# A decoder on one core: both layers' threads merged into one order each, two heads per cross score product, tails by query tile

## The chip, the core and the metric

One Trainium2 chip, one of its cores. The metric is the device time of one execution in microseconds, the median of the runs shown. One profiled execution gives the trace from which every row here is taken.

## What is computed

x is 8 sequences of 256 tokens with 256 features; ctx is 8 sequences of 77 tokens with 192 features. There are two layers, each sublayer followed by a residual and a layer norm:

```python
x = _layernorm(x + _L0_attn_ref(x, ...))        # gated linear attention, 4 heads, keys 64, values 128
x = _layernorm(x + _L0_xattn_ref(x, ctx, ...))  # cross attention, 16 heads of 16: x0
x = _layernorm(x + _L0_ffn_ref(x, ...))         # 8 experts, the top 2 of each token, hidden size 512
x = _layernorm(x + _L1_attn_ref(x, ...))        # self attention, 16 heads, window of 128 keys to either side: s1
x = _layernorm(x + _L1_xattn_ref(x, ctx, ...))  # cross attention, scores clipped at +-10000: x1
x = _layernorm(x + _L1_ffn_ref(x, ...))         # 8 experts, top 2, with a capacity for each expert
```

## The kernel before

The eight sequences are four pairs; sequence p of a pair is thread p (0 or 1), with its own buffers and its own four of the eight PSUM banks, `bank(p, 0)` to `bank(p, 3)`. A thread is a list of named stages, and a stage is a function of each engine that takes part in it. `in_turns` weaves the two threads into one order by a written list of turns (so many stages of thread 0, so many of thread 1, and so on); `play` (L225) runs through it on every engine, which issues the instructions of its stages in just that order. So the order says what is queued behind a waiting instruction on each engine. There is an order for each pair: TURNS0 and TURNS1 for the first three of a layer, LAST0 and LAST1 for the last, with routing steps (choose, count, rank, hots, table, place, index, gather) put in between. Between the layers come the experts of layer 0, after layer 1 its own.

The stages of one attention (x0, s1 or x1; `c` is which): `k`, `v`, `q` projections on TensorE, copied with bias by VectorE (`kz`, `va`) and ScalarE (`qe`); `scores` on TensorE in units, each followed by `max` on VectorE (L874 for s1 in 4 units of 4 heads; L878 for a cross attention in 2 units of one query tile and 16 heads). `split` and `nmT` turn the maxima round, and `ST` (L1630) makes the scores again, transposed and shifted, for `exp` on ScalarE (L645); x1 has `clip` on VectorE (L895) and `shift` in between. Then the tail: `values` (L1658, TensorE), `OT` (L649, ScalarE copies 1024 columns), `untr` (L1666, transposed back, 8 transposes), `norm` (L901, L903, VectorE), `tout` (L1673, 4 transposes), `onT` (L653, ScalarE), `wo` (L1680, projection), `res` (L910 and layer norm moments L833 to L840, VectorE), `rstd` (L1388, GpSimd), `final` (L846, VectorE). Heads lie in rows of 32, four groups beside each other (`rows_of(r)`).

A cross score unit:

```python
for g in range(G):
    for r in range(RT):
        ins = mm(bank(p, r)[:, g * M:(g + 1) * M], b.q[rows_of(r), g // 2, u * P:(u + 1) * P], kz[rows_of(r), g // 2, g % 2, :],
                 start=(g == 0), stop=True, skip_group_check=True)
if p == 1 and u == 0:
    ins = idle(p, IDLE_SCORES, 0, G * M)
```

`idle` (L1566) issues products whose result nobody reads. They stand at the split, at the clip, before the turn of the gated attention (thread 1), before the router's logits and in the last turn of a layer, besides the place above.

In layer 0 the gated attention of the pair comes first (`g_...`: keys, values and gates L1728, scores L1750, mix L1758 to L1760, turn L1775, output L1783), and the keys of the next pair (`g_keys`) are made in the tail of the cross attention.

Of the kernel before, what the change touches and what calls it, by code (L numbers as in the profile page):

```python
# [11 lines left out]
ALU = mybir.AluOpType  # L12
ACT = mybir.ActivationFunctionType
# [53 lines left out]
class Attn:  # L67
# [14 lines left out]
    def scores_at(self, n):  # L82

        if self is X0:
            return NT * n
        return NT * PAIRS + (G + NT) * n + (0 if self.selfattn else G)

    def exps_at(self, n):

        if self is X0:  # L90
            return KC * n
        return KC * PAIRS + (G + KC) * n + (0 if self.selfattn else G)
# [24 lines left out]
def cross_stages(c, clip):  # L117

    out = [("k", c), ("kz", c), ("v", c), ("va", c), ("turn", c), ("xinT", c), ("q", c), ("qe", c), ("xb", c)]
    for t in range(NT):  # L120
        out += [("scores", c, t), ("max", c, t)]
    out += [("split", c), ("nmT", c), ("nmTe", c)]
    for k in range(KC):
        out.append(("ST", c, k))
        if clip:
            out += [("clip", c, k), ("shift", c, k), ("exp", c, k)]
        else:
            out.append(("exp", c, k))
# [3 lines left out]
def after_probs(c):  # L132
    return [(n, c) for n in ("values", "OT", "untr", "norm", "tout", "onT", "wo", "res", "rstd", "final")]

def self_stages(c):
    out = [("xb", c)]
    for g in range(G):
        out += [("scores", c, g), ("max", c, g)]
    out += [("split", c), ("nmT", c), ("nmTe", c)]  # L140
    for g in range(G):
        out += [("ST", c, g), ("exp", c, g)]
    return out + after_probs(c)
# [6 lines left out]
def lockstep(n, stages):  # L150

    return [(s, p, n) for s in stages for p in range(2)]

def in_turns(n, threads, turns, extra):

    out, at = [], [0, 0]
    for i, count in enumerate(turns):
        p = i % 2
        for stage, m in threads[p][at[p]:at[p] + count]:  # L160
            if m < PAIRS:
                out.append((stage, p, m))
            out += [((e,), 0, n) for e in extra.get((p, *stage), [])]
        at[p] += count
    assert at == [len(t) for t in threads]
# [3 lines left out]
TURNS0 = (3, 3, 4, 2, 3, 4, 2, 3, 4, 2, 3, 4, 5, 7, 4, 1, 2, 4, 4, 4, 2, 1, 4, 4, 1, 2, 2, 2, 2, 2, 2, 2, 2, 1, 2, 7, 6, 3, 5, 4)  # L169
TURNS1 = (3, 3, 2, 2, 1, 1, 2, 2, 5, 5, 5, 5, 2, 2, 2, 2, 2, 2, 3, 3, 2, 1, 3, 4, 1, 5, 6, 2, 2, 3, 3, 2, 3, 1, 3, 5, 3, 3, 1, 1, 3, 3, 2, 1, 2, 3, 8, 3, 3, 5, 4, 7, 4, 4)  # L170
LAST0 = (2, 2, 2, 2, 6, 6, 2, 2, 3, 2, 6, 5, 5, 1, 2, 1, 3, 8, 3, 1, 2, 5, 5, 6, 2, 2, 3, 2, 2, 2, 7, 5, 4, 7, 3, 3)
# [1953 lines left out]
```

## Time and profile before

| | us |
|---|---|
| median of 3 runs | 1130.51 |
| lowest and highest | 1126.09, 1133.84 |
| span of the profiled execution | 1131.2 |
| TensorE busy in it | 1010.0 (89%) |
| VectorE busy | 618.1 (55%) |
| ScalarE busy | 425.0 (38%) |
| GpSimd busy | 255.4 (23%) |
| mean granted TensorE clock | 0.967 |

Layer 0 with its four pairs goes to about 381 us, its experts to 597, layer 1 to 1027, the experts of layer 1 and the end to 1131.
### The profile page before, as it was taken

To read this page: it belongs to the slowest core of one execution; us is meant where nothing else is said; L and a number is where in the kernel's file an instruction comes from. 1 tells how busy PE (TensorE), PEld (TensorE's weight loads), DVE (VectorE), ACT (ScalarE), POOL (GpSimd) and SP (SyncE) were. 2 spreads that over 40 slices of the span, in tenths; PEclk is the share of its full clock that TensorE was granted. 3 is DMA by queue.
4 is the path that set the end of the run, shared out by engine and by line. 5 is a ranking of instruction groups with operands and counts; after the bars stand their busy time and mean duration, and the time that the engine had idled before them with its cause. 6 is when DMAs were issued, how large, how long until landed. Compare 5 with 4: busy or idle time off the path is not lost.

```text
span 1131.2 us, 20802 instructions
## 1 busy us (share of the span) xinstructions
PE 1010.0 (89%) x8612; PEld 719.1 (64%) x8612; DVE 618.1 (55%) x1398; ACT 425.0 (38%) x557; POOL 255.4 (23%) x282
## 2 busy tenths in 40 slices
PE   6889889999987899999998798879888987986997
PEld 3666566576575799997445465747565665654566
DVE  2653753662667564333334846675575668765443
ACT  1533533524433355555541254142416231541112
POOL 0310310120130233333322020231013110210662
PEclk9999999899897899999999899999999999997999
DMA  6013413211400691111113000200020010004447
GB/s 188 1 43 126 135 43 107 89 43 44 152 1 1 254 378 57 47 48 47 43 39 98 1 2 6 85 2 5 1 76 2 6 38 1 1 2 131 130 135 236
DMA packets 64237, 80.50 MB, mean 71 GB/s; under 512 B 12736, under 2 KB 57680, under 8 KB 63120
## 3 DMA queue, kind: packets, MB, share of 16 engines
q1 hardware_dynamic: 53392, 61.15, 16.3%
q0 software_dynamic: 5664, 15.47, 4.2%
q10 hardware_dynamic: 5088, 2.56, 0.9%
q8 instruction: 68, 1.11, 0.4%
q14 instruction: 25, 0.20, 0.1%
HBM read 46.13 MB, written 33.03 MB: 70 GB/s over the span
## 4 chain that ended last, share of the span: by engine, by line
PE 61%; DVE 17%; ACT 12%; issue 5%; DMA 2%; POOL 2%; SPq 0%; ACTq 0%; DVEq 0%; POOLq 0%
PE ps L1522 8%; PE ps L1857 7%; DVE sb_arena L874 6%; ACT sb_arena L645 6%; PE ps L1658 5%; PE ps L1680 4%; PE ps L1885 4%; PE ps L1868 3%; PE ps L1728 3%; PE ps L1783 3%; DVE sb_arena L878 3%; PE ps L1566 2%; PE ps L1995 2%; PE ps L1630 2%; PE ps L1905 2%
## 5 line engine op out<-in xcount | busy, mean ns | idle before, releaser
L645 ACT ACTIVATE sb_arena<-ps 77x2048 f32<-77x2048 f32 (+1 forms) x64 | 116.5, 1880 | 27.9 <-PE ps L1612 26.7
L1388 POOL TENSOR_TENSOR sb_arena<-sb_arena,sb_neghalf 128x2 f32<-128x2 f32 x40 | 28.7, 719 | 397.2 <-DVE sb_arena L840 397.2
L1522 PE MATMUL ps<-sb_arena,sb_wreg 128*128 128x256 f32 (+1 forms) x512 | 110.8, 365 | 6.8 <-issue 3.8
L1522 PEld LDWEIGHTS ps<-sb_arena,sb_wreg 128*128 128x128 f32 (+1 forms) x512 | 89.0, 195 | 23.7 <-issue 8.3
L1857 PE MATMUL ps<-sb_arena 128*128 128x128 f32 x800 | 100.2, 280 | 3.2 <-ACT sb_arena L757 2.3
L1630 PE MATMUL ps<-sb_arena 32*77 32x256 f32 (+1 forms) x1024 | 78.4, 424 | 25.8 <-ACT sb_arena L645 13.1
L1857 PEld LDWEIGHTS ps<-sb_arena 128*128 128x128 f32 x800 | 97.0, 196 | 5.2 <-ACT sb_arena L757 2.9
L757 ACT ACTIVATE sb_arena<-sb_arena 128x1024 f32 x72 | 76.0, 1057 | 16.8 <-issue 12.4
L1630 PEld LDWEIGHTS ps<-sb_arena 32*77 32x77 f32 (+1 forms) x1024 | 44.3, 177 | 46.1 <-ACT sb_arena L645 24.2
L874 DVE TENSOR_REDUCE sb_arena<-ps 128x8 f32<-128x2048 f32 x32 | 71.0, 2282 | 3.5 <-PE ps L1586 3.5
L1566 PE MATMUL ps<-sb_headrow,sb_identb 128*32 128x512 bf16 (+1 forms) x266 | 65.8, 385 | 1.4 <-DVE sb_arena L878 1.3
L1465 POOL DMA_INDIRECT outs<-sb_arena,sb_idx x36 | 35.5, 987 | 134.8 <-ACT sb_arena L743 134.8
L901 DVE RECIPROCAL sb_arena<-ps 128x32 f32<-128x32 f32 x24 | 8.6, 357 | 100.2 <-PE ps L1666 98.7
L635 ACT ACTIVATE sb_nmTb<-ps 128x256 bf16<-128x256 f32 x24 | 9.2, 383 | 143.5 <-PE ps L1604 143.5
L1658 PE MATMUL ps<-sb_arena,sb_va 77*32 77x256 f32 (+1 forms) x1024 | 58.5, 381 | 3.1 <-ACT sb_arena L645 2.5
L1728 PE MATMUL ps<-sb_wreg,sb_arena 128*128 128x512 f32 x128 | 60.7, 635 | 0.2 <-DVE sb_arena L926 0.2
L1409 POOL TENSOR_SCALAR_AFFINE_SELECT sb_arena<-sb_arena 128x512 f32<-128x512 f32 x48 | 29.6, 647 | 125.2 <-ACT sb_arena L645 125.2
L878 DVE TENSOR_REDUCE sb_arena<-ps 128x16 f32<-128x1232 f32 x32 | 45.4, 1438 | 21.1 <-PE ps L1591 21.0
L846 DVE TENSOR_SCALAR sb_arena<-sb_arena 128x256 f32<-128x256 f32 x80 | 39.2, 531 | 27.3 <-POOL sb_arena L1388 27.1
L1680 PE MATMUL ps<-sb_wreg,sb_arena 128*128 128x256 f32 x192 | 45.2, 384 | 5.7 <-ACT sb_arena L653 5.7
L1658 PEld LDWEIGHTS ps<-sb_arena,sb_va 77*32 77x32 f32 (+1 forms) x1024 | 31.2, 110 | 27.4 <-ACT sb_arena L645 8.7
L1583 PE MATMUL ps<-sb_arena 32*128 32x256 f32 x512 | 36.7, 400 | 13.2 <-DVE sb_arena L874 13.2
(285 smaller groups left out, 1886.9 us busy)
## 6 DMA issues: line engine op xcount, KB each, us to landing
sb_arena<-in_m_w SPq DMA_DIRECT2D x8, 1536.0 KB, 9.8
sent<-sb_xres SPq DMA_DIRECT2D x32, 256.0 KB, 2.6
sb_arena<-outs SPq DMA_DIRECT2D x16, 512.0 KB, 6.0
outs<-sb_zeros SPq DMA_DIRECT2D x4, 1664.0 KB, 9.7
sent<-sb_zeros SPq DMA_DIRECT2D x2, 2560.0 KB, 13.7
sb_arena<-in_m_w SPq DMA_DIRECT2D x16, 256.0 KB, 3.4
early<-sb_xres SPq DMA_DIRECT2D x12, 256.0 KB, 2.9
sb_arena<-in_xT SPq DMA_DIRECT2D x8, 256.0 KB, 3.2
```

The lines of the kernel that those rows point to most:

```text
L645: nc.scalar.activation(dst, src, ACT.Exp).then_inc(S(f"h_PT{p}"), 1)
L757: nc.scalar.activation(arena[:, to:to + 1024], arena[:, bass.ds(blk * WORDS + 1024 * part, 1024)], ACT.Copy).then_inc(S(signal), 1)
L874: v.tensor_reduce(b.nm[:, :, u].rearrange("p (t r) -> p r t", t=NT), bank(p, 0, RT).rearrange("p r (t k) -> p r t k", t=NT), axis=AX.X, op ...
L878: v.tensor_reduce(b.nm[:, u * RT:(u + 1) * RT, :], bank(p, 0, RT)[:, :, 0:G * M].rearrange("p r (g k) -> p r g k", g=G), axis=AX.X, op=ALU ...
L1522: ins = mm(dst[:, m * cols:(m + 1) * cols], wt[0:rows, k, m * P:(m + 1) * P], src[0:rows, k, 0:cols], start=(k == 0), stop=(k == KC - 1))
L1566: ins = mm(bank(p, n)[IDLE:P, first:], identb[:, IDLE:P], headrow[:, :, :].rearrange("p g k -> p (g k)")[:, first:], start=True, stop=True ...
L1630: ins = mm(bank(p, r)[0:c.keys, a * L:(a + 1) * L], key, b.q[rows_of(r), u // 2 if c.selfattn else u, :], start=(a == 0), stop=False, skip ...
L1658: ins = mm(bank(p, 2 + g // 2)[rows_of(r), (g % 2) * L:(g % 2 + 1) * L], b.va[0:c.keys, kt, g * RT + r, :], b.PT[0:c.keys, g, first:first ...
L1680: ins = mm(bank(p, 3)[:, t * D:(t + 1) * D], bufs[p].onT[:, k, t * P:(t + 1) * P], W[f"{c.name}_wo"][:, k, :], start=(k == 0), stop=(k == ...
L1728: ins = mm(bank(p, 2 + t), b.xT[:, k, t * P:(t + 1) * P], W[wt][:, k, :], start=(k == 0), stop=(k == KC - 1))
L1857: ins = mm(to[:, m * P:(m + 1) * P], w[:, k, m * P:(m + 1) * P], slots0[j % 2].xT[:, k, :], start=(k == 0), stop=(k == KC - 1))
L1885: ins = mm(to[rows, :], slots0[j % 2].xT[:, k, rows], weights_of(c, blk, at + FH * k, FH, at + FH * k), start=(k == 0), stop=(k == KC - 1) ...
```

## The change

Four things. A cross score product now takes the two heads that share a chunk of the query together, so that a unit has 8 products of 154 columns for 16 of 77, and the unread products after thread 1's first cross scores are gone. The stages from `values` to `res` are split in two: `values` and `OT` by half of the head groups, `untr`, `norm`, `tout`, `onT`, `wo` and `res` by query tile. For that the results of tile 1 lie in bank 2 (`result_bank`) and the turned tile 1 in bank 1 (`turned_bank`), and the keys of the next pair in layer 0 wait for the residual. Each layer has one order for all four pairs (`whole_thread`, TURNS0 with 330 turns and TURNS1 with some 450, mostly of one to three stages), and the routing steps are put at new places of it; the early count goes to thread 1 and its banks. The other unread products stay where they were; those of the last turn of a layer now wait for the residual.

```diff
-                    for g in range(G):
+                    for k in range(KC):
                         for r in range(RT):
-                            ins = mm(bank(p, r)[:, g * M:(g + 1) * M], b.q[rows_of(r), g // 2, u * P:(u + 1) * P], kz[rows_of(r), g // 2, g % 2, :],
-                                     start=(g == 0), stop=True, skip_group_check=True)
-                    if p == 1 and u == 0:
-                        ins = idle(p, IDLE_SCORES, 0, G * M)
+                            ins = mm(bank(p, r)[:, 2 * k * M:2 * (k + 1) * M], b.q[rows_of(r), k, u * P:(u + 1) * P],
+                                     kz[rows_of(r), k, :, :].rearrange("p a m -> p (a m)"), start=(k == 0), stop=True, skip_group_check=True)
...
 def after_probs(c):
-    return [(n, c) for n in ("values", "OT", "untr", "norm", "tout", "onT", "wo", "res", "rstd", "final")]
+    out = []
+    for i in range(2):
+        out += [("values", c, i), ("OT", c, i)]
+    for n in (("untr", "norm"), ("tout", "onT"), ("wo", "res")):
+        for t in range(NT):
+            out += [(x, c, t) for x in n]
+    return out + [("rstd", c), ("final", c)]
...
+def whole_thread(head, thread, p):
+
+    return head + [(stage, m) for n in range(PAIRS) for stage, m in thread(p, n) if m < PAIRS]
...
+        def turned_bank(p, t):
+
+            return bank(p, 1 if t else 2)[:, 0:KC * P].rearrange("p (k q) -> p k q", k=KC)
+
+        def result_bank(p, t):
+
+            return bank(p, 2 if t else 3)[:, 0:D]
...
+            def heads(p, n, c, i):
+                act.wait_ge(S(f"h_OT_done{p}"), 2 * c.at(n) + i + 1)
+                nc.scalar.activation(bufs[p].OT[:, 2 * i:2 * i + 2, :], halves(bank(p, 2 + i)), ACT.Copy).then_inc(S(f"h_OT{p}"), 1)
...
+            def norm(p, n, c, t):
+                b = bufs[p]
+                dve.wait_ge(S(f"h_O{p}"), NT * c.at(n) + t + 1)
+                o = bank(p, t).rearrange("p (h x) -> p h x", x=2 * DH)
+                v.reciprocal(b.rec[:, t, :], o[:, :, DH]).then_inc(S(f"h_on{p}"), 1)
+                dve.wait_ge(S(f"h_on{p}"), 2 * (NT * c.at(n) + t) + 1)
+                v.tensor_tensor(b.on[:, t, :].rearrange("p (h x) -> p h x", h=H), o[:, :, 0:DH],
+                                b.rec[:, t, :].unsqueeze(2).broadcast_to([P, H, DH]), ALU.mult).then_inc(S(f"h_on{p}"), 1)
+
+            def residual(p, n, c, t):
+                b = bufs[p]
+                dve.wait_ge(S(f"h_wo{p}"), NT * c.at(n) + t + 1)
+                if t == 0:
+                    dve.wait_ge(S(f"h_xb{p}"), c.at(n) + 1)
+                v.tensor_tensor(b.res[:, t, :], result_bank(p, t), b.xb[:, t, :], ALU.add).then_inc(S(f"h_res{p}"), 1)
+                dve.wait_ge(S(f"h_res{p}"), NT * c.at(n) + t + 1)
+                ins = v.bn_stats(b.st1 if t else b.st0, b.res[:, t, :])
+                if t + 1 == NT:
+                    ins.then_inc(S(f"h_moments{p}"), 1)
+                    moments("h", p, c.at(n))
...
             def turn_result(p, n, c):
                 if n + 1 == PAIRS and p == 0:
+                    pe.wait_ge(S(f"h_res{p}"), NT * (c.at(n) + 1))
                     idle(p, IDLE_RESULT, 2)
...
             def gla_keys(p, n):
                 b = bufs[p]
                 pe.wait_ge(S(f"a_in{p}"), 64 * (n + 1))
+                if n:
+                    pe.wait_ge(S(f"h_res{p}"), NT * X0.at(n))
```

TensorE's order in pair 1 of layer 0, from the turn of the gated attention to the first scores, was: k0, g_turn0, g_turn1, g_wo0, g_wo1, k1, v0, turn0, v1, q0, turn1, q1, scores0.0, scores1.0, scores0.1, scores1.1. It is: k0, g_turn0, g_wo0, g_turn1, v0, g_wo1, k1, turn0, v1, q0, turn1, scores0.0, q1, scores0.1, scores1.0, scores1.1. In the tail of x1 it was untr0, untr1, tout0, wo0, (turn of the next pair), tout1, wo1; it is untr0.0, untr0.1, untr1.0, tout0.0, untr1.1, tout0.1, wo0.0, wo0.1, tout1.0, tout1.1, wo1.0, (turn of the next pair), wo1.1.

## Rows read from the trace of the kernel before

**Rows 1.** By stage: length, busy PE, PEld, DVE, ACT, POOL, clock, DMA, GB/s
```profile
110.00:197.00 87.00, 79.61 (x648) 56.23 (x648) 44.40 (x91) 35.49 (x53) 15.56 (x14) 1.00 0.31 101
197.00:287.00 90.00, 83.42 (x643) 58.33 (x644) 44.25 (x90) 35.17 (x52) 15.57 (x14) 0.94 0.23 74
287.00:381.00 94.00, 82.46 (x644) 56.75 (x642) 66.38 (x194) 35.20 (x52) 18.12 (x17) 0.88 0.17 58
...
726.00:829.00 103.00, 89.86 (x1021) 62.09 (x1020) 64.41 (x113) 36.84 (x40) 17.68 (x24) 1.00 0.09 27
```

**Rows 2.** The chain that ended last, in order of time: start, length, what
```profile
625.06 15.49 DVE sb_arena L874 x7
...
659.53 7.16 PE ps L1658 x128
...
730.70 15.49 DVE sb_arena L874 x7
...
762.80 7.16 PE ps L1658 x128
```

**Rows 3.** Timeline of TensorE: the tail of S1 in pair 1
```profile
769.85 2.31 PE L1666 MATMUL ps<-sb_ident,sb_arena 128*128 128x128 f32 x16
...
773.83 3.62 PE L1680 MATMUL ps<-sb_wreg,sb_arena 128*128 128x256 f32 x16
777.28 1.01 PE L1522 MATMUL ps<-sb_arena,sb_wreg 96*128 96x77 f32 x8
```

**Rows 4.** Timeline of TensorE: the tail of X1 in pair 1
```profile
809.02 2.31 PE L1666 MATMUL ps<-sb_ident,sb_arena 128*128 128x128 f32 x16
...
812.63 1.99 PE L1680 MATMUL ps<-sb_wreg,sb_arena 128*128 128x256 f32 x8 [0.69 <-ACT sb_arena L653]
...
816.23 1.99 PE L1680 MATMUL ps<-sb_wreg,sb_arena 128*128 128x256 f32 x8 [0.74 <-ACT sb_arena L653]
818.06 1.89 PE L1522 MATMUL ps<-sb_arena,sb_wreg 128*128 128x256 f32 x8
```

**Rows 5.** Timeline of TensorE: cross scores and tail of X0, pair 1
```profile
155.20 1.99 PE L1522 MATMUL ps<-sb_arena,sb_wreg 128*128 128x256 f32 x8 [0.69 <-ACT sb_arena L624]
...
157.12 2.13 PE L1591 MATMUL ps<-sb_arena 32*128 32x77 f32 x64
...
175.25 2.31 PE L1666 MATMUL ps<-sb_ident,sb_arena 128*128 128x128 f32 x16
...
182.78 1.04 PE L1709 MATMUL ps<-sb_arena,sb_wreg 128*16 128x256 f32 x4
```

**Rows 6.** Timeline of TensorE: products of 32 rows and 256 columns
```profile
792.85 1.10 PE L1630 MATMUL ps<-sb_arena 32*77 32x256 f32 x16 [0.47 <-ACT sb_nmTb L635]
```

**Rows 7.** Timeline of VectorE: maxima of the cross scores, X0, pair 1
```profile
158.32 4.21 DVE L878 TENSOR_REDUCE sb_arena<-ps 128x16 f32<-128x1232 f32 x3 [1.99 <-PE ps L1591]
```

**Rows 8.** Groups by line and form, whole span: busy, mean ns, idle before
```profile
L649 ACT ACTIVATE sb_arena<-ps 128x1024 f32<-128x1024 f32 x24 | 24.6, 1023 | 28.1 <-PE ps L1658 28.0
...
L903 DVE TENSOR_TENSOR sb_arena<-ps,sb_arena 128x512 f32<-128x512 f32 x24 | 16.6, 691 | 0.8
...
L653 ACT ACTIVATE sb_arena<-ps 128x512 f32<-128x512 f32 x24 | 14.3, 596 | 29.6 <-PE ps L1673 29.6
...
L743 ACT ACTIVATE sb_arena<-ps 128x256 f32<-128x256 f32 x36 | 13.8, 383 | 75.7 <-PE ps L1868 46.3 <-PE ps L1905 29.3
...
L901 DVE RECIPROCAL sb_arena<-ps 128x32 f32<-128x32 f32 x24 | 8.6, 357 | 100.2 <-PE ps L1666 98.7
...
L1332 DVE TENSOR_TENSOR sb_arena<-ps,sb_arena 128x256 f32<-128x256 f32 x16 | 6.1, 420 | 8.3 <-PE ps L1995 8.3
```

**Rows 9.** Timeline of TensorE: unread products in layer 1's last turn
```profile
1027.21 2.76 PE L1566 MATMUL ps<-sb_headrow,sb_identb 128*32 128x512 bf16 x12
```

**Rows 10.** Timeline of TensorE: unread products before the turn, thread 1
```profile
139.10 1.04 PE L1566 MATMUL ps<-sb_headrow,sb_identb 128*32 128x512 bf16 x4
```

**Rows 11.** Busy time in a stretch of 4 us, columns as in group 1
```profile
644.00:648.00 4.00, 2.81 (x28) 1.91 (x32) 2.46 (x10) 3.97 (x4) 0.35 (x1) 0.57 0.00 0
```

More of the change, by code:

```diff
@@ L147, in self_head, with in_turns @@
     return [(n, c) for n in ("turn", "xinT", "k", "kz", "q", "qe", "v", "va")]
-def lockstep(n, stages):
-    return [(s, p, n) for s in stages for p in range(2)]
-def in_turns(n, threads, turns, extra):
+def in_turns(threads, turns, extra):
     out, at = [], [0, 0]
@@ L187, in first_thread @@
         of_pair(n, "o_turn", "o_T") + of_pair(n + 1, "g_decay", "g_z") + of_pair(n, "o_route", "o_logits", "store")
[L190 to L198 removed]
+def whole_thread(head, thread, p):
+    return head + [(stage, m) for n in range(PAIRS) for stage, m in thread(p, n) if m < PAIRS]
+LAST = PAIRS - 1
+EXTRA0 = {(1, 3, "g_sp"): ["choose"], (1, 3, "g_y"): ["count", "counts"], (0, 3, "g_wo"): ["rank"], (0, 3, "OT", X0, 1): ["hots"],
+          (1, 3, "OT", X0, 0): ["table"], (0, 3, "res", X0, 1): ["index"], (0, 3, "rstd", X0): ["place"], (1, 3, "norm", X0, 0): ["raw"],
+          (0, 3, "final", X0): ["turned"], (1, 3, "norm", X0, 1): ["first"], (0, 3, "o_turn"): ["blocks", "gather"]}
+EXTRA1 = {(0, 3, "kz", S1): ["choose"], (1, 3, "va", S1): ["count", "counts"], (0, 3, "values", S1, 0): ["rank"], (0, 3, "values", S1, 1): ["hots"],
+          (0, 3, "rstd", X1): ["place"]}
+def first_layer():
+    head = of_pair(0, "g_keys", "g_low", "g_decay", "g_z")
+    return in_turns([whole_thread(head, first_thread, p) for p in range(2)], TURNS0, EXTRA0)
 def second_thread(p, n):
@@ L443, in build_program @@
         order0 = first_layer()
[L444 to L445 removed]
+        order1 = second_layer()
         def rows_of(r):
@@ L777, in _ @@
             act.wait_ge(S("rescaled"), 3)
-            play(head1, stages)
-            for order in order1:
-                play(order, second)
+            play(order1, second)
             picks(3, 4)
@@ L1309, in _ @@
             scale_bias(["s1_bq", "x1_bq"], "rescaled")
-            play(head1, stages)
-            for order in order1:
-                play(order, stages | routing(1))
+            play(order1, stages | routing(1))
             choose_late(1)
@@ L1475, in store1 @@
                     unread(p)
-            play(head1, stages)
-            for order in order1:
-                play(order, stages | {"store": lambda p, n: store1(p, n)})
+            play(order1, stages | {"store": lambda p, n: store1(p, n)})
             def gather1(e):
```

167 lines of the change are left out of this document (67 added, 100 removed), and 16 rows, old and new, of tables (TURNS0, TURNS1).

## The prediction

> **What bounds the kernel now.** I read the busy time by stage first. In a pair of layer 1 (726 to 829 us) TensorE is busy 89.9 of 103 us, VectorE 64.4, ScalarE 36.8; in a pair of layer 0 (110 to 197 us) TensorE 79.6 of 87 [rows 1]. So TensorE is the engine to look at, but it waits 13 and 7 us in a pair, and the chain of work that ended last, in order of time, says for whom. From 730.70 us VectorE takes 15.49 us for seven of the eight S1 maxima (2.2 us each) and TensorE waits for it; then ScalarE runs eight exponentials of 1.9 us; the value products start at 762.80 us, and from there TensorE and the hand-overs between engines set the time [rows 2]. The edits don't touch the maxima or the exponentials. They touch the cross scores and what follows the values, so the sum is one of TensorE's waits there.
>
> The row that matters most is the tail, the stretch from the end of the values to the end of the output projection. In S1, pair 1, it runs from 769.85 to 777.28 us [rows 3]: 7.43 us. TensorE's own work in it is 16 transposes back (about 1.8), 8 transposes out (0.9) and 8 projections (773.83 to 777.28, 3.45), 6.2 us; 1.2 us is waiting for copies and normalisations. In X1 it runs from 809.02 to 818.06 us, 9.04 us [rows 4], for the same work and one early turn of the next pair (0.45): 6.7 us, so 2.3 us of waiting, of which 0.69 and 0.74 are named there. In X0 175.25 to 182.78 us, 7.53 us [rows 5].
>
> **Part 1, two heads per cross score product.** Each of the 32 score units (2 layers, 4 pairs, 2 threads, 2 query tiles) had 16 products of 77 columns and now has 8 of 154, with half the weight loads. Two units took 2.13 us in 64 records, 33 ns a record, 1.06 us a unit [rows 5]. A product of the same 32 rows with 256 columns takes 1.10 us for 16 records, 69 ns [rows 6]. On the line between them 154 columns take 48 ns, so 16 records take 0.77 us: 0.29 less. The bounds: nothing (the time goes by columns, which stay 1232) and 0.53 less (it goes by records). I take 0.29, because 77 columns lie close to the line's lower end and the price can't be wholly by columns when 3.3 times the columns cost 2.1 times the time. Most of it is hidden: VectorE needs 4.21 us for three maxima with nothing between [rows 7], longer than the scores either way. Only the first unit of a phase stands ahead of VectorE. So 0.29 in each of 8 phases. The 4 unread products after thread 1's first cross scores go as well; they ran while thread 0's maximum was on VectorE, so they are worth nothing here, but see the clock.
> The page "TensorE: Matmul & The Clock Gate" of the Trainium skill (LDWEIGHTS, loading the stationary operand) says that a weight load takes time by its columns, whatever its rows. By that the old unit is bound by its loads of 128 columns, and halving them would save the whole 0.53, 2 us more over the eight phases; no row here separates loads from products.
>
> **Part 2, tails by query tile.** Values, copy, transposes back, normalisation, transposes out, copy, projection and residual become two each. The work of TensorE stays. ScalarE's copy of OT, 1.02 us for 1024 columns, becomes two of 0.60; onT's 0.60 becomes two of 0.38; VectorE's 0.69 us operations on 512 columns become two of 0.42, the reciprocal of 0.36 two of between 0.18 and 0.36 [rows 8]. That adds 0.34 us of ScalarE and some 0.4 to 0.7 us of VectorE to each of 24 tails, 8 us and 10 to 17 us in all, beside TensorE's 6.2 us of work a tail. If that cover were gone, VectorE's part alone would be 0.7 us a tail.
> I set the new S1 tail on the old one's clock, t = 0 at 769.85. Thread 1's first OT copy is over while its second value half runs; the second copy ends at 0.75 instead of 1.15. Transposes back of thread 0 fill 0 to 0.9, of thread 1's tile 0 to 1.35. Thread 0's tile 0 is normalised at 1.3 (0.03 + 0.25 + 0.42 after 0.5), tile 1 at 2.05, thread 1's tiles at 2.75 and 3.5. Transposes out and projection follow each: thread 0's tile 0 is projected from 3.0, the four halves (0.87 each) and the last transposes end near 6.7. Old: 7.43. So 0.7 us a tail; what is late next, thread 1's final, has its residual and half of its statistics done earlier by the same amount, and the K and V products of X1 (3.4 us) still cover it. X0, the same from 7.53: 0.8. In X1 the new order also puts all of thread 0's tail before thread 1's transposes out, and thread 1's last projection after the early turn. The same working ends at 7.3 against 9.04: 1.7. The last pair is another matter: after its projection stand the place products and 12 unread products (2.76 us) that now wait for the residual first [rows 9], so what the tail gives is cut: 0.9.
>
> **Part 3, the merged orders.** Most of TensorE's sequence is the old one, as the two lists of stages for pair 1 show, read against each other. Two things differ in layer 0. The scores of thread 0 now stand ahead of thread 1's Q, in a wait of 0.69 us [rows 5]. By the durations in the rows its first maximum starts 2.5 us sooner than at 158.32; each thread's second maximum then waits for its own scores, 1.1 and 0.9 us, and the 0.3 us of the split fall into these waits: 0.75 is left at the end of the maxima. The output projection of the gated attention, thread 0, stands ahead of thread 1's four unread products and turn; these took 1.04 us inside a wait [rows 10] and are now in the way, and thread 0's projection waits 1.1 us for its copy: it costs about 0.5. The new waits (keys of the next pair on the residual, since its tile 1 lies in bank 2) are passed while thread 1's projections (1.8 us) run, the residual needing 0.5; g_low, decay and all of ScalarE's next pair are queued behind it and so don't move. DMA: no transfer is added; the loads still wait on the same events. The count moves to thread 1, inside VectorE's work in both layers: nothing. In the last pair of layer 0 the 64 one-hots and the table stay on VectorE ahead of thread 1's norm, but thread 0's exponentials and values pass ahead of thread 1's: I take the 1.05 of the other pairs and 0.75 more for this, a choice without a row of its own (its ends are nothing and one exponential, 1.9).
>
> **Sum.** Layer 0: 3 pairs x (0.75 - 0.5 + 0.8) = 3.2, last pair 1.8. Layer 1: 3 pairs x (0.7 + 0.29 + 1.7) = 8.1, last pair 0.7 + 0.29 + 0.9 = 1.9. Together 15. The profiled execution spans 1131.2 us, the median is 1130.5, so 0.7 is taken off: 1130.5 - 15 = 1115.5, say 1116. The clock is left as it is in this sum.
>
> **The rivals.**
> (a) The clock falls in the cross scores; this one ends on the other side. TensorE runs mostly at 1.2 GHz (granted 0.57) at 644 us [rows 11], just behind the S1 maxima of pair 0, in which it waits for VectorE. Pair 1 of either layer shows 1.00 throughout [rows 1]. After the change TensorE does some 1.2 us less there and the unread products are gone, so it stands still about as much as in the S1 maxima. The price: pair 0 of layer 1, with such a fall, takes 34.5 us from its first maximum to its values (625.06 to 659.53), pair 1 32.1 [rows 2]: 2.4 us. In all eight phases that is 19 us: 1135. It outweighs the gain from seven phases on. For it: the same S1 stretch did not fall in pair 1 and did in pair 0, so little decides. Against it: the four unread products at the split and those at the clip stay. The Trainium skill, same page, Part 1, has the clock fall after a stretch of little activity; the trace agrees in the direction, at 644 us.
> (b) The tails give little: each half is a hand-over more, and what I save before the projection is lost at the final, which waits for GpSimd anyway. Then only part 1 and the X1 order are left, 2.3 and 4 x 0.7 = 2.8: 1125. For it: so many halves that each of my waits of 0.1 us counts; against it: the named waits of 0.69 and 0.74.
> (c) The half-clock stretches of layer 0 go. Its pairs 2 and 3 (197 to 287 and 287 to 381 us) average 0.94 and 0.88 and take 3 and 7 us more than pair 1. If new timing spares them, another 10: 1106. For it: pair 1 has the same work as pair 2, at 1.00 [rows 1].
>
> **How the numbers follow.** The forecast, 1116, 50%; (a) 15%, half of it only partly, near 1125; (b) 20%; (c) 15%. A measurement of this kernel can tell about 1%, so faster means under 1119.2. The forecast with its own range of 1109 to 1123 is under it with 0.7 of its 50%, (c) wholly, (b) and (a) with little: 0.35 + 0.15 + 0.05 = 0.55. Over 1141.8 only the worst of (a), where a fall costs more than 2.4: 0.05. The rest, 0.4, lies within 1%. The range leaves out the ends of (a) and (c): 1103 to 1131.
>
> **What would show it.** L1591 in 512 records of about 48 ns pitch, and the first maximum 0.3 us earlier behind Q. The S1 tail at 6.7 us, X1's at 7.3, the layer 1 pair at 100.5 instead of 103.2. The S1 maxima and exponentials unchanged. Granted clock 1.00 in the cross scores of the steady pairs; if it is near 0.5 there, (a) holds and this forecast is wrong. If pairs of layer 1 stay over 102 us at full clock, (b).

## The result

| kernel | median (runs) | against before | span x granted clock | the rest |
|---|---|---|---|---|
| before | 1129.35 us (4) | 1 | 1097.7 us | 30.7 us |
| after | 1142.97 us (4) | 1.0136 [1.0089, 1.0184] | 1080.3 us | 62.3 us |

The change is slower by 1.4%; the forecast was 1116 us, with a chance of 5% for a time over 1141.8. The last two columns are worked out from the span and the mean granted clock that each run lists (means over the 4 runs of after, and over the 56 listings of before that came with the first eight experiments): span times clock is what would be left if every cycle of TensorE came at 2.4 GHz; the rest is what stretches at 1.2 GHz add. It is a rough split: waiting in such a stretch counts as cycles too, and the clock has three decimals, about 1 us of one execution. It says in one line what happened: at full clock the change takes 17 us out; the clock puts 32 back. A second measurement of the same kernel, beside other runs of before, gave 1.0141 [1.0092, 1.0191] and 16.7 us less against 31.6 more. In all that follows the ratios leave out executions in a slower state of the chip (two of e6_route, one of e5_alt, and one of e16_merged_tails that took 1212.75 us), while medians and splits hold all of a kernel, so a ratio isn't just the quotient of two medians.

The profiled execution of after took 1139.87 us (span 1138.1). Its busy time by stage, the same stages as in [rows 1], columns as there:

```profile
115.00:210.00 95.00, 87.10 (x573) 58.72 (x572) 45.44 (x96) 35.89 (x56) 15.47 (x14) 0.87 0.27 86
210.00:306.00 96.00, 88.09 (x581) 59.70 (x580) 45.41 (x96) 35.87 (x56) 15.46 (x14) 0.88 0.22 71
306.00:404.00 98.00, 82.82 (x579) 54.85 (x579) 67.48 (x200) 36.08 (x57) 19.63 (x18) 0.87 0.18 65
742.00:843.00 101.00, 88.26 (x956) 60.76 (x955) 65.79 (x122) 37.76 (x48) 18.10 (x24) 1.00 0.10 31
```

Read the clock column (the third from the end) against [rows 1]. Pair 1 of layer 0 was 87 us at 1.00 and is 95 at 0.87; pair 2 was 90 at 0.94 and is 96 at 0.88. A pair of layer 1 holds 1.00 and is 2 us shorter. The loss is not in the amount of work but in the clock, and most of it in layer 0. Adding up one minus the clock over steps of 4 us, the profile of before loses 20.5 us up to 400 us and 12.3 in layer 1 (620 to 1048 us), that of after 42.7 and 7.2; a second profile of after has 44.3 and 10.9.

Layer 1 did what was forecast. The chain of work that ended last, in order of time, the rows that answer to [rows 2] (start, length, what), and behind them the row of before that ends its pair, of which [rows 2] has the start:

```profile
747.07 15.49 DVE sb_arena L893 x7
...
779.17 7.11 PE ps L1682 x128
...
847.41 15.49 DVE sb_arena L893 x7
```

```profile
833.94 15.49 DVE sb_arena L874 x7
```

From 747.07 to 847.41 us are 100.3 us, where before has 103.2, from 730.70 to 833.94 (forecast: 100.5); seven maxima still take 15.49 us. TensorE's timeline, the tail of X1 in pair 1 (start, length, engine, line, tiles; in brackets the idle time before and what ended it):

```profile
824.25 1.53 PE L1690 MATMUL ps<-sb_ident,sb_arena 128*128 128x128 f32 x12
825.72 0.44 PE L1696 MATMUL ps<-sb_ident,sb_arena 128*128 128x128 f32 x2
825.99 0.60 PE L1690 MATMUL ps<-sb_ident,sb_arena 128*128 128x128 f32 x4
826.42 0.38 PE L1696 MATMUL ps<-sb_ident,sb_arena 128*128 128x128 f32 x2
826.64 1.98 PE L1702 MATMUL ps<-sb_wreg,sb_arena 128*128 128x256 f32 x8
828.46 0.60 PE L1696 MATMUL ps<-sb_ident,sb_arena 128*128 128x128 f32 x4
829.31 1.13 PE L1702 MATMUL ps<-sb_wreg,sb_arena 128*128 128x256 f32 x4 [0.25 <-ACT sb_arena L669]
830.28 0.60 PE L1540 MATMUL ps<-sb_ident,sb_arena 128*128 128x128 f32 x4
830.72 1.03 PE L1702 MATMUL ps<-sb_wreg,sb_arena 128*128 128x256 f32 x4
831.58 1.76 PE L1546 MATMUL ps<-sb_arena,sb_wreg 128*128 128x256 f32 x7
```

From the first transpose back to the next pair's first K product it is 7.33 us, against 9.04 in [rows 4] (forecast: 7.3); the two waits of 0.69 and 0.74 are one of 0.25. The tail of S1, 786.22 to 792.88 us, is 6.66 us against 7.43 in [rows 3] (forecast: 6.7); that of X0 in pair 1, 189.77 to 196.54 us, 6.77 against 7.53 in [rows 5] (forecast: 6.7).

Layer 0 did not. TensorE's timeline in the X0 scores of pair 2; L1616 are the score units, L1653 the products that make them again (x16 are records, two for each float32 product):

```profile
262.24 0.81 PE L1616 MATMUL ps<-sb_arena 32*128 32x154 f32 x16
262.99 1.99 PE L1546 MATMUL ps<-sb_arena,sb_wreg 128*128 128x256 f32 x8
264.92 0.81 PE L1616 MATMUL ps<-sb_arena 32*128 32x154 f32 x16
265.91 0.81 PE L1616 MATMUL ps<-sb_arena 32*128 32x154 f32 x16 [0.19 <-ACT sb_arena L644]
268.63 1.11 PE L1616 MATMUL ps<-sb_arena 32*128 32x154 f32 x16 [1.91 <-DVE sb_arena L897]
269.67 1.89 PE L1589 MATMUL ps<-sb_headrow,sb_identb 128*32 128x512 bf16 x4
271.50 0.40 PE L1627 MATMUL ps<-sb_identb,sb_nmb 128*128 128x128 bf16 x2
272.36 2.00 PE L1653 MATMUL ps<-sb_arena 32*77 32x256 f32 x16 [0.47 <-ACT sb_nmTb L650]
```

Thread 0's two units and thread 1's first are through at 266.7; thread 1's second has to wait 1.91 us until VectorE has read the first. Before, the longest wait between these units was

```profile
251.46 1.13 PE L1591 MATMUL ps<-sb_arena 32*128 32x77 f32 x32 [0.29 <-DVE sb_arena L878]
```

Behind the 1.91 us, sixteen records of products of 256 columns take 2.00 us where [rows 6] has 1.10, and four unread products 1.89 where [rows 10] has 1.04. The clock in steps of 3 and 4 us (columns as in [rows 1]):

```profile
266.00:269.00 3.00, 1.09 (x25) 0.86 (x28) 2.86 (x4) 0.00 (x0) 0.00 (x0) 1.00 0.00 0
269.00:272.00 3.00, 2.89 (x22) 0.92 (x14) 1.81 (x3) 0.07 (x1) 0.00 (x0) 0.50 0.02 5
272.00:276.00 4.00, 3.16 (x30) 1.76 (x34) 0.00 (x0) 1.16 (x3) 0.00 (x0) 0.50 0.00 0
276.00:280.00 4.00, 3.77 (x50) 2.30 (x42) 0.00 (x0) 3.23 (x3) 0.00 (x0) 0.60 0.00 0
```

That is 1.2 GHz for some 10 us. And ahead of the same pair's scores, in the turn of the gated attention (L1800 the turn, L1808 the output projection, L1589 unread products):

```profile
241.90 1.97 PE L1800 MATMUL ps<-sb_ident,sb_arena 128*128 128x128 f32 x8 [0.57 <-POOL sb_arena L1482]
244.98 5.46 PE L1808 MATMUL ps<-sb_wreg,sb_arena 128*128 128x256 f32 x16 [1.11 <-ACT sb_arena L726]
250.37 1.04 PE L1589 MATMUL ps<-sb_headrow,sb_identb 128*32 128x512 bf16 x4
```

Eight projections (16 records) take 5.46 us; the same group in the last pair, at full clock (336.40 us), takes 3.73, although the same wait of 1.11 stands ahead of it. Both profiles of after show clocks under 1 at the same places of pairs 0 to 2: the gated turn (52 to 60, 144 to 156, 240 to 249 us), the X0 scores (from 76, 172 and 268 us), the route behind X0 (108 to 124, 208 to 220 us). Before has of these only the route of pairs 1 and 2 (196 to 208 and 284 to 296 us) and a short fall at the gated turn of pair 2 (228 to 232). In the last pair both kernels fall, before at 320 to 324, 344 to 360 and from 380 us, after at 356 to 372 and 376 to 391. So the order sets where the clock falls, for the most part: the second profile of after has one fall more in layer 0, in the route of pair 2 (304 to 316 us).

### The profile page after: what moved, and what is told of

It is laid out like the page before. It is cut to its first block, busy times and chain, and to the rows that moved or that the text cites. A ratio compares the mean times of both kernels' runs of the same rounds, so it can differ in the third digit from the quotient of the medians.

```text
span 1138.1 us, 19839 instructions
## 1 busy us (share of the span) xinstructions
PE 1012.4 (89%) x8068; PEld 710.5 (62%) x8068; DVE 630.4 (55%) x1470; ACT 431.5 (38%) x605; POOL 256.0 (22%) x282
## 4 chain that ended last, share of the span: by engine, by line
PE 64%; DVE 19%; ACT 11%; POOL 2%; issue 2%; DMA 2%; SPq 0%; ACTq 0%; DVEq 0%; POOLq 0%
PE ps L1882 7%; PE ps L1546 7%; ACT sb_arena L660 7%; DVE sb_arena L893 6%; PE ps L1682 5%; PE ps L1753 4%; PE ps L1910 3%; PE ps L1893 3%; PE ps L1702 3%; PE ps L1653 3%; PE ps L1589 3%; PE ps L1808 3%; DVE sb_arena L897 2%; PE ps L2018 2%; PE ps L1930 2%
## 5 line engine op out<-in xcount | busy, mean ns | idle before, releaser
L1653 PE MATMUL ps<-sb_arena 32*77 32x256 f32 (+1 forms) x1024 | 83.2, 445 | 26.1 <-ACT sb_arena L660 14.0
L1653 PEld LDWEIGHTS ps<-sb_arena 32*77 32x77 f32 (+1 forms) x1024 | 46.1, 185 | 48.1 <-ACT sb_arena L660 24.6
L920 DVE RECIPROCAL sb_arena<-ps 128x16 f32<-128x16 f32 x48 | 12.0, 250 | 105.2 <-PE ps L1690 105.2
L1589 PE MATMUL ps<-sb_headrow,sb_identb 128*32 128x512 bf16 x234 | 63.5, 413 | 1.7 <-DVE sb_arena L897 1.6
L1702 PE MATMUL ps<-sb_wreg,sb_arena 128*128 128x256 f32 x192 | 48.3, 394 | 1.0 <-ACT sb_arena L669 1.0
```

What stands on the lines that cost most here:

```text
L1589: ins = mm(bank(p, n)[IDLE:P, first:], identb[:, IDLE:P], headrow[:, :, :].rearrange("p g k -> p (g k)")[:, first:], start=True, stop=True ...
L1653: ins = mm(bank(p, r)[0:c.keys, a * L:(a + 1) * L], key, b.q[rows_of(r), u // 2 if c.selfattn else u, :], start=(a == 0), stop=False, skip ...
L1702: ins = mm(result_bank(p, t), bufs[p].onT[:, k, t * P:(t + 1) * P], W[f"{c.name}_wo"][:, k, :], start=(k == 0), stop=(k == KC - 1))
```

## The experiments

Theory W: layer 0's new order leaves TensorE waiting at places where the clock then falls. Theory F: the clock falls because the four unread products after thread 1's first cross scores are gone, or because the products of two heads are thinner. Short names: "turn" is thread 0's copy and gated projection behind thread 1's turn, as in pairs 0 to 2 before; "scores" is thread 0's first X0 scores behind thread 1's Q and the four units of the two threads by turns, as before. All ratios are to the kernel before, measured beside. What a profile shows is one execution of each.

| run | median | ratio, 95% | span x clock | rest |
|---|---|---|---|---|
| e1_fill | 1145.6 | 1.0149 [1.0122, 1.0177] | 1083.2 | 59.9 |
| e2_turn | 1132.4 | 1.0004 [0.9972, 1.0036] | 1080.9 | 48.0 |
| e3_scores | 1135.0 | 1.0051 [1.0030, 1.0072] | 1087.9 | 45.6 |
| e4_both | 1126.8 | 0.9961 [0.9936, 0.9986] | 1084.7 | 41.2 |
| e5_alt | 1135.0 | 1.0038 [1.0003, 1.0073] | 1080.0 | 53.2 |
| e6_route | 1133.4 | 0.9999 [0.9964, 1.0033] | 1088.0 | 41.8 |
| e7_old0 | 1127.7 | 0.9976 [0.9951, 1.0002] | 1086.5 | 39.9 |
| e8_two_heads | 1125.2 | 0.9963 [0.9945, 0.9982] | 1096.8 | 26.9 |
| e9_old_layer0 | 1122.9 | 0.9960 [0.9933, 0.9988] | 1085.7 | 35.9 |
| e10_fill | 1119.2 | 0.9909 [0.9887, 0.9931] | 1089.2 | 28.4 |
| e11_no_unread | 1130.3 | 1.0008 [0.9981, 1.0035] | 1091.9 | 36.3 |
| e12_last | 1116.0 | 0.9893 [0.9865, 0.9921] | 1085.4 | 29.6 |

The last four ran beside a kernel before of 1135.5 us (1101.4 and 32.4): e13_last_fill 1120.2, 0.9877 [0.9860, 0.9893]; e15_gated_filled 1137.6, 1.0013 [0.9995, 1.0030] (1089.3 and 46.8); e16_merged_tails 1129.3, 0.9943 [0.9926, 0.9959]; e17_after_again 1151.3, 1.0141 [1.0092, 1.0191] (1084.7 and 64.1). They are compared by their ratios alone.

**e1_fill.** In scores(), cross part:

```diff
+                    if p == 1 and u == 0:
+                        ins = idle(p, IDLE_SCORES, 0, G * M)
```

> The changed kernel with the four unread products after thread 1's first cross scores put back, in both layers; nothing else. Theory F (the clock falls in the cross scores of layer 0 because these products are gone): granted clock back near 1.00 in the X0 scores of pairs 0 to 2, each pair about 5 us shorter there, 1143 falls to about 1128. Theory W (the order of layer 0 makes TensorE wait, 1.9 us behind the scores and 1.1 us for the copy ahead of the gated projection): the four products run ahead of the 1.9 us wait and shorten it to about 1, so at most the scores stretch improves by a few us, the gated stretch stays at half clock, layer 0 pairs stay over 92 us, total 1136 to 1144.

Measured: 1.0149. The unread products alone do nothing for the changed kernel: the wait ahead of thread 1's second unit is 1.53 us for 1.91, and the clock still falls behind it in pairs 0 to 2. Theory F's first half falls as the cause of what layer 0 lost; its second half, the thinner products, falls with e8_two_heads below.

**e2_turn, e3_scores, e4_both.** A function that takes a thread's stages out of the merged list and puts them behind a stage of the other:

```diff
-    return in_turns([whole_thread(head, first_thread, p) for p in range(2)], TURNS0, EXTRA0)
+    out = in_turns([whole_thread(head, first_thread, p) for p in range(2)], TURNS0, EXTRA0)
+    for n in range(PAIRS):
+        out = behind(out, n, "0.g_yT", "1.g_turn")            # e2, e4
+        out = behind(out, n, "0.scores.x0.0", "1.q.x0")       # e3, e4
+        out = behind(out, n, "0.scores.x0.1", "1.max.x0.0")   # e3, e4, e5
+    return out
```

> The changed kernel with, in all four pairs of layer 0, thread 0's copy and projection of the gated attention behind thread 1's turn and its four unread products, as the kernel before has it in pairs 0 to 2. Theory W: clock 1.00 in this stretch, each pair about 4 us shorter; the X0 scores still fall; total about 1143 - 12 = 1131. Theory F, or that the fall has its cause in an earlier stage: the clock still falls here and the time stays within 3 us of 1143.

> The changed kernel with the X0 scores of layer 0 in the order of the kernel before (thread 0's first scores behind thread 1's Q, and the threads' units in turns), in all four pairs; the unread products stay out. Theory W: clock 1.00 in the X0 scores, each pair about 5 us shorter, the gated stretch still falls; total about 1143 - 15 = 1128. Theory F: the fall in the X0 scores stays, total within 3 us of 1143.

> Both order edits of the two kernels before this one together. Theory W: layer 0 pairs at 86 to 87 us with clock 1.00, pair periods of layer 1 still 100.5, total about 1143 - 27 = 1116. Theory F: within 5 us of 1143. If the cause is the rest of the merged order (route, tails): layer 0 stays over 92 us a pair, total over 1133.

Measured: 1.0004, 1.0051 and 0.9961. The edits give back 1.3%, 0.9% and together 1.8% (theory W had 1131, 1128 and 1116 us, so "scores" gave 8 us for the 15 expected), while span x clock grows by 1 to 8 us (1080.9, 1087.9 and 1084.7 against 1080.3): what they give is clock, and more than that. The units by turns, in pair 2 of e3_scores (L1637 are the scores, L918 the maxima, L1610 unread products):

```profile
257.32 0.81 PE L1637 MATMUL ps<-sb_arena 32*128 32x154 f32 x16
258.32 0.81 PE L1637 MATMUL ps<-sb_arena 32*128 32x154 f32 x16 [0.19 <-ACT sb_arena L665]
259.69 0.81 PE L1637 MATMUL ps<-sb_arena 32*128 32x154 f32 x16 [0.56 <-DVE sb_arena L918]
261.04 0.81 PE L1637 MATMUL ps<-sb_arena 32*128 32x154 f32 x16 [0.54 <-DVE sb_arena L918]
262.39 1.04 PE L1610 MATMUL ps<-sb_headrow,sb_identb 128*32 128x512 bf16 x4 [0.54 <-DVE sb_arena L918]
```

Three waits of half a microsecond stand where one of 1.91 was, and the four unread products take 1.04 us: 2.4 GHz. But e2_turn disturbs the simple story: its scores are those of after, wait included, and the clock held in pairs 0 and 1. Its row in pair 1, and the stretch after it:

```profile
165.58 0.81 PE L1635 MATMUL ps<-sb_arena 32*128 32x154 f32 x16 [1.91 <-DVE sb_arena L916]
```

```profile
164.00:168.00 4.00, 1.99 (x22) 0.99 (x22) 3.32 (x6) 0.38 (x1) 0.00 (x0) 1.00 0.00 0
168.00:172.00 4.00, 3.04 (x54) 1.94 (x58) 0.30 (x2) 2.38 (x3) 0.00 (x0) 1.00 0.00 0
```

The same wait of 1.91 us stands ahead of a fall in each of pairs 0 to 2 of after and in one of them here (256 to 260 us, 0.59). So one wait doesn't decide; what went before it may. Units by turns are no guarantee either: in e4_both the clock fell at them in pair 1 (168 to 172 us, 0.57). And e4_both, at 1126.8, is still 11 us over the forecast; the runs from e5_alt to e12_last look for them.

These profiles show something else. In those of e2_turn and e4_both the clock also falls in layer 1, which the edits don't touch: 18.5 and 18.3 us are lost from 620 to 1048 us, against 7.2 and 10.9 in the two of after. And in e2_turn, e3_scores and e4_both it falls at 24 to 28 us, ahead of everything that was edited, in neither of after. The medians of up to ten executions carry the argument, then, and single places of one profile only illustrate it.

**e5_alt.** e4_both without the line for "1.q.x0": the units by turns, but thread 0's first unit stays ahead of thread 1's Q.

> As e4_both (changed kernel, thread 0's gated projection behind thread 1's turn, X0 score units of the threads in turns), but thread 0's first X0 scores stay ahead of thread 1's Q, as in the changed kernel. If the fall of the clock in the X0 scores comes from the order of the four score units (the second of thread 0 ahead of the first of thread 1, which leaves a 1.9 us wait behind them): clock 1.00 there, and the 0.75 us a pair of the early first maximum is kept, 1124 to 1127, not slower than e4_both (1126.8). If it comes from the scores standing ahead of Q: the fall is back in pairs 0 to 2, total like e2_turn, 1132.

Measured: 1.0038 against e4_both's 0.9961. At full clock it is 4.7 us less than e4_both, 1.2 us a pair, more than the 0.75 of my Part 3; the clock takes 12 us more. The early scores do start VectorE earlier, and TensorE stands still later. Pair 1 in its profile:

```profile
162.25 1.33 PE L1637 MATMUL ps<-sb_arena 32*128 32x154 f32 x32 [0.93 <-ACT sb_arena L665]
164.63 1.41 PE L1637 MATMUL ps<-sb_arena 32*128 32x154 f32 x16 [1.04 <-DVE sb_arena L918]
```

Behind waits of 0.93 and 1.04 us, and none of 1.91, the clock fell in all of pairs 0 to 2 (76 to 80, 164 to 168 and 256 to 260 us, 0.58 to 0.60), as the expectation has it for scores ahead of Q. A wait needn't be near 2 us long for a fall to stand behind it.

**e6_route.** e4_both with IDLE_ROUTE 4 instead of 2.

> e4_both with four unread products instead of two ahead of each thread's router product in pairs 0 to 2 of layer 0 (twelve more, 0.27 us each: 3.2 us). TensorE isn't waiting there, yet the clock fell in it in all three pairs of e4_both (108 to 120, 200 to 216, 292 to 304 us; about 3.4 to 5 us each), behind products of 8 columns and of 16 rows. If unread products hold the clock there: full clock in the three stretches, 11 to 13 less and 3.2 more, about 1126.8 - 9 = 1118. If they don't: 1126.8 + 3 = 1130.

Measured: 0.9999 against e4_both's 0.9961; span x clock is 3.3 us more, the price of the twelve products, and the rest is the same (41.8 and 41.2). The falls in the route stretch (108 to 120, 200 to 212 and 292 to 304 us) are all there. Their cause is not known; TensorE is busy without a gap in them and ahead of them, with products of 16 rows and of 8 columns. The DMA engines move some 340 GB/s there, but they do so in pair 0 of before as well (104 to 120 us), at a clock of 1.00, so they alone don't make the fall.

**e7_old0, e9_old_layer0, e12_last.** The changed kernel with TURNS0 of before for pairs 0 to 2 of layer 0 (e7), LAST0 of before for its last pair too (e9); tail stages in two halves one behind the other, layer 1 as changed. e12 is e9 with the three lines of e4 for the last pair, which the kernel before ordered otherwise.

> The changed kernel with pairs 0 to 2 of layer 0 in the order of the kernel before, each tail stage in its two halves one behind the other; the last pair of layer 0 and layer 1 as in the changed kernel. Theory W (what layer 0 lost is the new order): pairs 0 to 2 of layer 0 like before (86 to 90 us), layer 1 at 100.5, total about 1130 - 10 = 1120 or, if the last pair of layer 0 keeps what it lost there, 1124. If the split of the tails or the two-head products cost something in layer 0: over 1130.

> As e7_old0, and the last pair of layer 0 too in the order of the kernel before (its order of the routing steps as well), each tail stage in two halves; layer 1 as in the changed kernel. If the last pair's new order is where 3 us at full clock and some of the clock go: 286 us from the first X0 maximum of pair 3 to the first S1 maximum instead of 293, total 1127.7 - 6 = 1121. If the last pair loses by its split tails: stays at 290 or more, total 1126 to 1129.

> e9_old_layer0 with the last pair of layer 0 ordered like pairs 0 to 2 of the kernel before in two places: thread 0's gated projection behind thread 1's turn, and the X0 score units behind thread 1's Q and in turns. The kernel before itself lost the clock in the last pair at 344 to 360 us, behind a wait of 1.53 us in the unturned score units. By theory W that fall goes (3 us or more at its 1.2 GHz): about 3 us less than e9_old_layer0, 1118. If the fall has another cause (hots and table on VectorE, whose rows follow): the same time as e9_old_layer0.

Measured: 0.9976, 0.9960 and 0.9893. The rest goes from 62.3 us in after to 39.9, 35.9 and 29.6, before's own 30 to 31: layer 0's new order is what cost most of the clock. e7 is 4 to 8 us slower than expected, and e9 can't be told from it by the intervals; e12 can be told from both. From the first X0 maximum of the last pair to the first S1 maximum the profiles have 293.2 us in e7, 283.7 in e9 and 281.6 in e12 (before 286.4, after 292.3). e12_last, at 1116.0 us, is faster than both kernels; its median over six executions is at the forecast, but it is another kernel, without layer 0's merged order. Its stages (pairs 1, 2 and the scores and tail of 3 of layer 0, then a pair of layer 1):

```profile
160.00:247.00 87.00, 77.76 (x584) 54.51 (x588) 45.27 (x97) 35.73 (x56) 15.56 (x14) 1.00 0.24 78
247.00:339.00 92.00, 82.21 (x580) 56.99 (x572) 51.72 (x125) 35.83 (x56) 15.56 (x14) 0.94 0.19 61
339.00:378.00 39.00, 28.53 (x318) 19.79 (x318) 30.07 (x116) 13.17 (x19) 5.31 (x7) 0.96 0.17 65
722.00:823.00 101.00, 88.26 (x963) 60.62 (x965) 67.48 (x125) 37.76 (x48) 18.11 (x24) 1.00 0.08 23
```

Pair 1 is at 1.00 again, as in [rows 1], and layer 1 has its 101 us.

**e8_two_heads, e11_no_unread.** The kernel before with the two-head products of the diff alone (e8), and also without its four unread products (e11).

> The kernel before with two heads per cross score product and nothing else (its orders, whole tails and unread products stay). By my sum 0.29 us in each of 8 phases: 1130.1 - 2.3 = 1128. If a weight load of 128 columns had bound the old unit: 1126. If the sparser stream of products makes the clock fall: half-clock stretches in the X0 and X1 scores, 1133 or more.

> e8_two_heads (the kernel before with two heads per product) with the four unread products of the cross scores left out. If they were worth nothing (my forecast): 1125.2 within 1.5. If they held the clock in the cross scores of this order: half-clock stretches in X0 or X1 scores and 1129 or more.

Measured: 0.9963, and 1.0008 without the unread products. Part 1 by itself is worth 4 to 5 us, and the thinner products don't lower the clock (rest 26.9 for 30.8 beside it). The four unread products are worth 5 us in this order (two intervals that just touch): without them span x clock is 4.9 less, and the rest 9.5 more. I had put them at nothing. Where the clock is lost isn't seen: the profile of e11_no_unread is of an execution of 1124.1 us, and its X0 scores in pairs 0 to 2 are at full clock.

**e10_fill, e13_last_fill.** e9_old_layer0 and e12_last with the lines of e1_fill.

> e9_old_layer0 with the four unread products of the cross scores put back in both layers. If they hold the clock anywhere: the clock's loss is smaller and the time 2 to 6 us less than e9_old_layer0. If they don't (as in e1_fill): the same within 2 us, or 1 to 3 us more, since in X1 and X0 they may stand ahead of thread 0's second scores.

> e12_last with the four unread products of the cross scores put back. If they hold the clock in turned score units, as e8 to e11 and e9 to e10 showed (4 to 5 us): 1112 to 1114. If e12_last has no fall left that they could prevent: 1116 to 1119, their own 0.5 us in each place being on the path.

Measured: 0.9909 against 0.9960 of e9, a gain of half a per cent; 0.9877 against 0.9893 of e12, no difference that the intervals tell. So the same four products are worth 5 us, 4 us or nothing, by the order around them.

**e15_gated_filled.** The changed kernel, with unread products in the wait for the copy. gla_out():

```diff
+                if p == 0:
+                    idle(p, 4, 1)
                 pe.wait_ge(S(f"gla_act{p}"), GLA_ACT.done("yT", n))
```

> The changed kernel with four more unread products ahead of thread 0's gated projection in layer 0, inside its wait of 1.1 us for the copy; nothing else. If this wait makes the clock fall: no fall, or a shorter one, at 52 to 60, 144 to 155 and 240 to 252 us, 3 us each, total 1143 - 8 = 1135 or less. If the fall comes from what stands ahead of it (in pairs 1 and 2 it began before the wait): the same falls, 1141 to 1146.

Measured: 1.0013 against 1.0141 of the changed kernel beside it, 1.3% or 14 us for sixteen products that nobody reads; the intervals are far apart. The rest is 17 us less (46.8 for 64.1), span x clock 5 more. This is the run that shows with the order left alone that TensorE's standing still costs the clock: one wait of 1.1 us, filled in four pairs, gives back over half of the 32 us. The gated turn of pair 2, to be read against the one above:

```profile
233.56 1.09 PE L1800 MATMUL ps<-sb_ident,sb_arena 128*128 128x128 f32 x8 [0.57 <-POOL sb_arena L1482]
234.58 1.04 PE L1589 MATMUL ps<-sb_headrow,sb_identb 128*32 128x512 bf16 x4
235.76 3.73 PE L1810 MATMUL ps<-sb_wreg,sb_arena 128*128 128x256 f32 x16
```

The projections take 3.73 us again; pair 0 is at full clock too. In pair 1 the clock had fallen ahead of the filled wait, as it did in after, and came back sooner:

```profile
144.26 1.97 PE L1800 MATMUL ps<-sb_ident,sb_arena 128*128 128x128 f32 x8 [0.57 <-POOL sb_arena L1482]
146.16 1.66 PE L1589 MATMUL ps<-sb_headrow,sb_identb 128*32 128x512 bf16 x4
```

And the X0 scores of pairs 0 to 2, which weren't touched and still have their wait of 1.91 us, hold the clock too; pair 1:

```profile
166.00:186.00 20.00, 15.48 (x239) 9.73 (x239) 6.99 (x15) 11.54 (x14) 0.00 (x0) 1.00 0.01 2
```

A fall is thus not bound to its own wait: with one filled, falls behind others went as well. It isn't as simple as one wait for one fall, though. This profile, the slowest of ten executions (1145.9 us), also has falls that after has not, at 24 to 28 us and at the gated turn of the last pair (324 to 328), and loses 20.2 us in layer 1 for 7.2; up to 400 us it loses 27.3 for the 42.7 and 44.3 of after. Which falls go, in a usual execution, it can't say. The 1.91 us wait itself was not filled. Its eight banks are those that VectorE is reading or that hold scores to be read; the Trainium skill ("PSUM — Partial Sum Buffer", PSUM bank collisions raise a hardware error) has TensorE's write and another engine's read of one bank as an error, and no run here tries it.

**e16_merged_tails.** e12_last with pairs 0 to 2 of layer 0 as in e4_both.

> e12_last with the merged order of the changed kernel in pairs 0 to 2 of layer 0 (tail halves of the threads interleaved, next pair's keys early), but thread 0's gated projection behind thread 1's turn and the X0 score units in turns, as in e4_both. If the last pair alone separates e4_both (1126.8) from e12_last (1116.0): 1116 to 1118. If the merged tails lead to falls of the clock in the route stretch (112 to 124 us): 1121 or more, with falls in three pairs there.

Measured: 0.9943, against 0.9893 of e12_last and 0.9961 of e4_both. The merged order of pairs 0 to 2 (its tails above all, but the places of the gated stages too) costs 0.5% against halves one behind the other. By the ratios that is most of what separates e4_both from e12_last; the intervals of e16 and e4_both overlap. Its profile is of the execution of 1212.75 us, so the place isn't known.

**e17_after_again.**

> The changed kernel again, unchanged, for a second profile and more executions beside these. If its falls of the clock in layer 0 are set by the order: the same stretches at half clock (gated turn, X0 scores, route in pairs 0 to 2), 1143 within 2 us. If they come and go between executions: other stretches, and a spread over 10 us.

Measured: 1.0141; the falls at the same places and one more, as told under the result. The four executions spread over 12 us (1143.9 to 1155.8), so both halves of the expectation have something: the order sets most places, and executions still differ.

## Why the prediction was wrong

- **The sum of work was right where it was worked out from rows.** Part 2 and layer 1: S1 to X1 maxima 55.1 us for 56.1 (forecast 1.0 less), X1 to S1 45.2 for 47.1 (forecast 1.7 less). Rival (b) is out. That the whole kernel came to 17 us at full clock for a sum of 15 is in part luck: 3 to 5 of the 17 are the run time of the unread products that were dropped (e1_fill against after, e8 against e11), which the sum had at nothing.
- **Part 1: the unit was right, its worth over the kernel was not.** A unit starts its successor after 0.75 us (262.24 to 262.99) instead of 1.06, 0.31 less for the forecast 0.29. The prediction's estimate by the Trainium skill ("TensorE: Matmul & The Clock Gate", LDWEIGHTS), that a weight load takes time by its columns, was 0.53 less; the trace disagrees. Alone (e8_two_heads) it brought 4.6 us for 2.3: span x clock fell by 0.8, less than forecast, and the rest by 3.9. The clock again.
- **"They are worth nothing here" (the unread products) was wrong** for the order of before, 5 us, and right for the changed one. I had looked at whether they delayed anything, and not at what they kept up.
- **"The clock is left as it is in this sum" is the step that failed.** Rival (a) had the mechanism and gave 1135 at 15%, but I put it into the cross scores of both layers and priced it at 2.4 us a place. What was added came in layer 0, at the scores, the gated turn and the route, up to 5 us a place in pairs 0 to 2; the rest grew by 32 us in all. X1's scores, which stand by turns, kept 1.00 in pairs 0 to 2 of the profile of after (in the second one they fell once, at 708 to 712 us). What the runs showed in place of a clock left as it is: layer 0's old order gives the 32 us back but for some 6 (e9_old_layer0, rest 35.9 for 62.3), and one filled wait gives 17 of them (e15_gated_filled).
- **Part 3 was read for waits and not for what follows them.** I wrote down TensorE's wait for the copy (1.1 us), but behind the early scores only VectorE's waits (1.1 and 0.9); that TensorE stands still for 1.91 us there I did not work out, and what I had I priced by its length. At full clock the prices were not far off: 1.2 us a pair gained by early scores (e5_alt against e4_both, forecast 0.75), and nothing to be seen for the projection (1080.3 us in after, 1080.9 in e2_turn; forecast 0.5 a pair lost). In time the order of the scores costs 8 us over the kernel (e3_scores) and that of the projection 11 (e2_turn).
- **The last pair of layer 0 had the wrong sign.** Forecast 1.8 us gained; from the first X0 maximum to the first expert product it went from 44.6 to 52.8 us. The clock explains some 6 of these 8: it is 0.74 over the 52.8 us and 0.83 over the 44.6, 13.7 us lost for 7.6. For the rest the profile of after names a wait:

```profile
395.19 2.00 PE L1702 MATMUL ps<-sb_wreg,sb_arena 128*128 128x256 f32 x8 [0.26 <-ACT sb_arena L669]
397.03 0.95 PE L1724 MATMUL ps<-sb_r,sb_arena 128*128 128x8 f32 x8
400.52 0.66 PE L1715 MATMUL ps<-sb_ident,sb_arena 128*128 128x128 f32 x4 [2.54 <-DVE sb_arena L865]
```

  Thread 1's projection is now wholly behind thread 0's twelve unread products and turn, only thread 0's router products (0.95 us) are left to cover its final, and TensorE waits 2.54 us; before it waited 1.43 at this place (378.74 us). That "thread 0 passes ahead" also means thread 1 comes last and alone was not in the sum.
- **Open.** Why the clock falls in the route stretch without a gap, and why four unread products there don't hold it; in pairs 1 and 2 of after it fell while the gated turn ran (from about 146.1 and 241.7 us), ahead of the wait that e15 filled. Why layer 1 lost 7 and 11 us in the profiles of after and 17 to 20 in those of e2_turn, e4_both, e5_alt, e6_route and e15_gated_filled, with the same layer 1, is open too. A rival that no run separates is that the fall depends on the moment as well as on the waits, so that any edit which shifts layer 0 by some us moves falls about; e15_gated_filled, whose products fit into the wait and shift nothing at full clock, speaks for the waits, and the falls at 24 to 28 us in some profiles only speak for the moment.

## What to carry to other kernels

Price a reordering twice: the work at full clock, and the places where TensorE stands still for a microsecond or two, with what the clock did behind such places; where both orders wait equally long in sum, try short waits by turns before one long (0.9% here). Before dropping products that nobody reads, ask what keeps the clock up in their place, and measure them in the order in which they will stay. When the parts of a change live in different stages, time them apart: here layer 1's part, layer 0's two-head scores, its tails in halves and a mended last pair give 1.1% together, and the whole change loses 1.4%.

## What the runs showed of the hardware

- What is done in one wait is felt later: four products of 0.26 us in a wait of 1.1 us, in each of four pairs, took 14 us off the kernel (e15_gated_filled); in its profile the X0 scores some 20 us further on hold the clock behind their unchanged wait, while a fall at the filled place itself went in pairs 0 and 2 only.
- Of pairs 0 to 2 of layer 0, the same wait of 1.91 us was followed by 1.2 GHz in three in after, in one in e2_turn and in none in e15_gated_filled. Waits of 0.93 and 1.04 us were, in three of three in e5_alt.
- The clock also fell where TensorE was busy throughout (108 to 120 us of e4_both, e6_route): in e4_both from about 110.2 us, behind products of 16 rows (106.85 and 108.50) and with the first ones of 8 columns (110.09).
- Executions of one kernel differ by 5 (e12_last) to 16 us (e5_alt), in e2_turn from 1121.7 to 1136.6, and with them the mean granted clock (0.968 to 0.953): one profile isn't the kernel.
- A score unit takes 0.75 us as 16 records of 154 columns and 1.06 us as 32 of 77, with the same 32 rows: neither the columns nor the number of weight loads alone sets the time.
